# Typed rows as three bf16 terms, one-hots laid side by side, 11 of 24 groups gathered in the build, spread stores, out-degrees from a fourth product

## The chip, the cores and the metric

One core of a Trainium2 chip runs the whole program in one launch. The metric is the device time of one execution in microseconds (us); lower is better.

## The reference

A graph network of four layers runs over 6,250 nodes with 128 features and 206,250 edges, which come sorted by destination. An edge has a source, a destination, one of 3 types, a weight and 64 features of its own.

```
L0: agg  = [relu(x), for t in 0..2: segment_sum(relu(x[src] @ W_e[t].T + b_e[t]) where type == t, dst)]
    x    = layernorm(x + (agg @ W_n[ntype].T + b_n[ntype]) + x)
L1: sup  = proj(mobius_add(logmap0(x) @ W, bias));  agg = segment_sum(edge_weight * sup[dst], src)
    x    = layernorm(x + proj(expmap0(agg)))
L2: deg  = segment_sum(1, src) + 1
    x    = layernorm(x + x / deg + segment_sum(rsqrt(deg[src] * deg[dst]) * x[src], dst))
L3: agg  = segment_sum(edge_attr @ W_edge + x[src], dst) * deg_in ** -0.5
    x    = layernorm(x + relu(agg @ W + bias))
```

## The kernel before

Nodes are cut into NB = 49 blocks of 128. The sums over edges are made in two ways. For L1 to L3 the kernel **builds** the adjacency once, plain in bf16 (`adj`) and weighted in float32 (`wadj`), in DRAM, and multiplies with it. For L0 and the edge features it goes over the edges in **groups**. The stages follow one another, each with its own order on each engine:

**Up to 287 us**: loads, in-degrees by a histogram (DVE one-hots in `hist_hot`, L317 and L318; PE products), and the fields of every edge (key, destination, weight, source, ...) written to `edge_fields`.

**Table stage, 287 to 569 us** (L892 to L1063). First the out-degree histogram of the sources: 101 batches (`outs`, L948 to L951), 44 of them ahead of everything (`AHEAD`), the rest shared out over 62 blocks. Then per block n (62; the first 49 carry typed messages): POOL fetches the block's edge fields by one gather (`took`, L919), ACT copies slot and weight (L998) and DVE picks valid slots (L966), PE transposes three tables, ACT evicts them as bf16 (L1005), DVE splits the weight in three bf16 parts, and SP stores `slot_tabs` (L899, 160 KB). PE multiplies a block of x with the three W_e (L1036 to L1040), ACT applies relu (L1015), and SP stores 128 rows of `typed_msgs` (3 x 128 float32).

**Build, 569 to 2199 us** (L1066 to L1173). A block is 8 batches of 16 slices; there are 62 blocks, 496 batches. A slice is a product of two one-hots over 128 edges: slot (128 columns) by source block (49 columns), once plain and three times times a weight part. Per batch DVE makes them in five operations (L1132 to L1137: `hi`, `lo`, `hi` times w1, w2, w3), all laid [4 slice groups][column][4 slices], so that PE's operands (L1155 to L1157) have a stride of four elements (8 bytes). PE does 3 products a slice: 98 columns (plain and w1), 49 (w2), 49 (w3). ACT evicts in two copies a batch (L1169, L1171). At a block's end SP stores `adj` (1568 KB) and `wadj` in four stores of 784 KB, each from 32 neighbouring partitions (L1107), then loads the next tables. POOL has nothing to do. Buffers are doubled by batch (one-hots, psum) and by block (stores).

**Edge stage, 2248 to 4427 us** (L1176 to L1327). There are NG = 856 groups of GE = 256 edges (U = 2 tiles of 128), in Q = 8 buffers; a group's rows all belong to one block of 128 destinations. SP loads a group's fields and features (L1255, L1257). POOL gathers its source rows of its type, one indirect DMA for 128 rows of 512 B (L1272). DVE makes the one-hots: 384 columns (type and destination) float32 for each tile (L1292) and 128 columns for the features (L1295), and adds the group's sums to `acc` (L1301) and `sum_e` (L1303). PE does two products of the features (L1315, float32, 128 columns) and two of the gathered rows (L1319, float32, 384 columns).

**The rest**: L0's node products and norm (to about 4704 us), the product with `wadj` for L1 (to 5362; its rows are `spread` over 4 by `spread_out`, L1543), two products with `adj` for L2 and L3 (L1743, 5436 to 6568), and the end at 6689.

Of the kernel before, what the change touches and what calls it, by code (L numbers as in the profile page):

```python
# [16 lines left out]
F32 = mybir.dt.float32  # L17
# [20 lines left out]
U, Q = 2, 8  # L38
GE = U * P
NG = -(-((E + NB * (GE - 1)) // GE) // Q) * Q  # L40
TP = NG * U
STEPS = NG // Q
# [15 lines left out]
KT = 8192  # L58
assert KT > NP + P
# [19 lines left out]
NO_ROW = OVR - 1  # L79
GB = JB + NB  # L80
# [4 lines left out]
HROW = AROW // S2  # L85

# [25 lines left out]
ROUNDS = 15  # L112
PEELED = NG // Q % ROUNDS


def in_groups(eng, step):

    for r in range(PEELED):
        step(r * Q)
    with eng.Fori(PEELED * Q, NG - ROUNDS * Q + 1, ROUNDS * Q) as g0:  # L120
        for r in range(ROUNDS):
            step(g0 + r * Q)


def build(nc, x, src, dst, attr, etype, weight, ntype, w_e, b_e, w_n, b_n, w1, b1, w3, w3e, b3, out):
    ctx = ExitStack()
    with ctx:
# [15 lines left out]
        typed_msgs = nc.dram_tensor("typed_msgs", (NP, T * D), F32, kind="Internal").ap()  # L143
        slot_tabs = nc.dram_tensor("slot_tabs", (GB * P, 5 * SLOTS), BF16, kind="Internal").ap()
# [14 lines left out]
        iota = sb("iota", T * P)  # L159
# [13 lines left out]
        start_of = sb("start_of", NG, I32, rows=1)  # L173

# [7 lines left out]
        ramp = sb("ramp", P * TU, BF16)  # L182
        big_words = (nc.sbuf_bytes_remaining // 4) // 16 * 16 - 64
# [69 lines left out]
        xTs, mrows = [room(D) for _ in range(2)], [room(T * D) for _ in range(2)]  # L253
# [48 lines left out]
        s_mst = sems("s_mst", 2)  # L302
# [35 lines left out]
        out_count = ps[5][:, 64:64 + NB]  # L338

        with nc.Block() as block:  # L340
            @block.sync
            def _(sp):
# [7 lines left out]
                for col, a in ((dst_i, dst), (src_i, src), (typ_i, etype), (w_c, weight)):  # L350
# [5 lines left out]
                sp.wait_ge(s_fillf, 9)  # L356
# [5 lines left out]
                sp.dma_start(by_place[E:BROWS, :].rearrange("(p u) r -> p (u r)", u=U),  # L362
                             fillf[0:(BROWS - E) // U, :]).then_inc(s_pads, 16)
# [5 lines left out]
            def _(pool):  # L369
# [3 lines left out]
                pool.iota(iota[:, :], pattern=[[KT, T], [1, P]], base=0, channel_multiplier=0,  # L373
# [6 lines left out]
                          allow_small_or_imprecise_dtypes=True).then_inc(s_cst, 1)  # L380
                pool.wait_ge(s_cst, 7)
# [117 lines left out]
            def _(dve):  # L499
# [9 lines left out]
                for f3, k in ((fillf.rearrange("p (u r) -> p u r", u=U), NO_NODE), (front.unsqueeze(1), -1)):  # L509
                    dve.memset(f3[:, :, KEY:DST + 1], float(k)).then_inc(s_fillf, 1)  # L510
# [32 lines left out]
                do(dve.scalar_tensor_tensor(F3[:, :, KEY], tmp, float(KT), F3[:, :, DST], ALU.mult, ALU.add))  # L543
# [331 lines left out]
        def slots_here(eng, n):  # L875
# [1098 lines left out]
```

## Time and profile before

| | |
|---|---|
| median of 3 runs | 6698.84 us (6689.83 to 6706.6) |
| profiled execution | 6690.94 us; its span 6689.2 us; granted clock 0.930 |
| PE busy | 5658.0 us (85%) |
| weight loads busy | 3702.9 us (55%) |
| DVE busy | 4679.1 us (70%) |
| POOL busy | 1809.4 us (27%) |
| ACT busy | 1031.0 us (15%) |
| DMA | 1028.57 MB, mean 154 GB/s |

The shares are means over stages with different limits: the build is full on PE and DVE while POOL is idle, and the edge stage has POOL at work and ACT idle. So it has to be read stage by stage.

### The profile page before, as it was taken

The numbers are of one execution on the slowest core, as the hardware profiler recorded it, in microseconds if no ns is written. First come the engines' busy times: TensorE is split into PE (matmuls) and PEld (weight loads), VectorE is DVE, ScalarE is ACT, GpSimd is POOL, SyncE is SP. The second block draws the span as 40 slices with busy tenths as digits, with TensorE's granted clock in tenths as the row PEclk, the third lists the DMA queues.
The fourth block names the chain that finished last, engine by engine and source line by source line (L and its number), as shares of the span: only waits on it lengthen the run. The fifth ranks groups of instructions, "written<-read, shape, count | busy, mean of one in ns | idle before, by whom it ended". The sixth has DMA issues, their size and how long they took to land. (4 is left out here: it accounts for less than half of the span.)

```text
span 6689.2 us, 122051 instructions
## 1 busy us (share of the span) xinstructions
PE 5658.0 (85%) x41983; PEld 3702.9 (55%) x41983; DVE 4679.1 (70%) x10318; ACT 1031.0 (15%) x1894; POOL 1809.4 (27%) x1887
## 2 busy tenths in 40 slices
PE   4398999999999688888888888874899959968896
PEld 3257999999999444444444444443555524433344
DVE  7789999999999788888888888868566650032003
ACT  0044444444444000000000000013000010000000
POOL 0011000000000477777777777720000002000200
PEclk5578999999999899999999999997999979989996
DMA  9555777777777433333333333340888737635862
GB/s 316 148 170 170 192 189 193 184 196 191 190 193 185 111 82 83 82 83 83 83 83 82 82 82 83 80 35 0 324 306 304 283 119 192 192 124 193 190 203 69
DMA packets 559193, 1028.57 MB, mean 154 GB/s; under 512 B 187721, under 2 KB 447710, under 8 KB 549578
## 3 DMA queue, kind: packets, MB, share of 16 engines
q1 hardware_dynamic: 486760, 872.14, 44.0%
q0 software_dynamic: 65392, 145.28, 9.7%
q10 hardware_dynamic: 6622, 6.38, 0.3%
q8 instruction: 162, 2.65, 0.2%
q14 instruction: 257, 2.11, 0.1%
HBM read 688.67 MB, written 387.65 MB: 161 GB/s over the span
## 5 line engine op out<-in xcount | busy, mean ns | idle before, releaser
L1272 POOL DMA_INDIRECT big<-typed_msgs,big x1712 | 1644.7, 961 | 2220.2 <-DMA big<-edge_fields 1729.8
L1319 PE MATMUL psum<-big 128*128 128x384 f32 x3424 | 1343.8, 515 | 331.0 <-DMA big<-typed_msgs,big 328.9
L1155 PE MATMUL psum<-big 128*128 128x98 bf16 x7936 | 1549.0, 272 | 49.2 <-DVE big L1137 38.2
L1156 PE MATMUL psum<-big 128*128 128x49 bf16 x7936 | 1535.7, 229 | 0.2 <-issue 0.2
L1157 PE MATMUL psum<-big 128*128 128x49 bf16 x7936 | 1534.8, 230 | 0.0
L1743 PE MATMUL psum<-big 128*128 128x512 bf16 (+1 forms) x4704 | 1003.1, 376 | 186.8 <-DMA big<-adj 186.8
L1319 PEld LDWEIGHTS psum<-big 128*128 128x128 f32 x3424 | 583.7, 190 | 756.6 <-DMA big<-typed_msgs,big 502.0
L1155 PEld LDWEIGHTS psum<-big 128*128 128x128 bf16 x7936 | 933.3, 118 | 104.1 <-DVE big L1137 78.3
L1156 PEld LDWEIGHTS psum<-big 128*128 128x128 bf16 x7936 | 945.1, 119 | 0.0
L1157 PEld LDWEIGHTS psum<-big 128*128 128x128 bf16 x7936 | 932.1, 117 | 0.3 <-issue 0.3
L1743 PEld LDWEIGHTS psum<-big 128*128 128x128 bf16 x4704 | 463.3, 99 | 721.9 <-DMA big<-adj 191.9
L1580 PE MATMUL psum<-big 128*128 128x416 f32 x1984 | 656.2, 494 | 61.5 <-DVE big L1614 60.8
L1292 DVE TENSOR_SCALAR big<-iota,big 128x384 f32<-128x384 f32 x1712 | 667.6, 430 | 2.4
L1315 PEld LDWEIGHTS psum<-big 128*64 128x64 f32 x3424 | 353.0, 136 | 535.5 <-issue 465.6
L1315 PE MATMUL psum<-big 128*64 128x128 f32 x3424 | 561.0, 287 | 64.9 <-DVE big L1295 52.8
L1133 DVE TENSOR_TENSOR big<-ramp,big 128x2048 bf16<-128x2048 bf16 x496 | 604.7, 1219 | 0.0
L1295 DVE TENSOR_TENSOR big<-iota,big 128x256 f32<-128x256 f32 x856 | 363.4, 425 | 335.2 <-PE psum L1319 329.9
L1614 DVE STREAM_TRANSPOSE big<-big 128x3136 f32<-128x3136 f32 x124 | 427.2, 3445 | 238.5 <-PE psum L1580 221.6
L1580 PEld LDWEIGHTS psum<-big 128*128 128x128 f32 x1984 | 378.0, 191 | 339.2 <-issue 82.3
L1169 ACT CAST big<-psum 128x784 bf16<-128x784 f32 x496 | 402.9, 812 | 870.0 <-PE psum L1157 870.0
L1790 POOL DMA_INDIRECT big<-spill,spill_row x98 | 92.5, 943 | 1502.0 <-DMA spill<-big 1472.7
L1301 DVE TENSOR_TENSOR big<-psum,big 128x384 f32 x856 | 471.6, 551 | 10.6 <-PE psum L1319 5.7
(294 smaller groups left out, 4630.4 us busy)
## 6 DMA issues: line engine op xcount, KB each, us to landing
wadj<-big SPq DMA_DIRECT2D x248, 784.0 KB, 13.0
big<-wadj SPq DMA_DIRECT2D x124, 1568.0 KB, 7.2
big<-adj SPq DMA_DIRECT2D x210, 896.0 KB, 4.7
adj<-big SPq DMA_DIRECT2D x62, 1568.0 KB, 5.3
big<-edge_feats SPq DMA_DIRECT2D x856, 64.0 KB
edge_feats<-in_edge_attr SPq DMA_DIRECT2D x1, 51562.5 KB, 163.2
big<-typed_msgs,big POOLq DMA_INDIRECT x1712
big<-edge_fields SPq DMA_DIRECT2D x856, 8.0 KB
```

Of the source, the lines that this page charges most:

```text
L1133: dve.tensor_tensor(lo_b[:, q, :, :, :], ramps(0, P), along_t(sl, P), ALU.is_equal)
L1155: pe.matmul(to[:, 0:2 * NB], lo, hi_b[:, q, g, :, u], start=True, stop=False)
L1156: pe.matmul(to[:, NB:2 * NB], lo, w2_b[:, q, g, :, u], start=False, stop=False)
L1157: last = pe.matmul(to[:, NB:2 * NB], lo, w3_b[:, q, g, :, u], start=False, stop=True)
L1272: pool.indirect_dma_start(out=got4[:, h, u, :], out_offset=None, in_=typed_rows, in_offset=bass.IndirectOffsetOnAxis(ap=fld4i[:, h, u, IDX ...
L1292: dve.tensor_scalar(hot4[:, h, u, :], iota[:, :], rel3[:, 0, h, u:u + 1], None, ALU.is_equal)
L1301: dve.tensor_tensor(to, ps[h][:, 0:T * P], to, ALU.add)
L1315: pe.matmul(ps[h][0:FE, T * P:(T + 1) * P], feat4[:, h, u, :], hotd4[:, h % LAG, u, :], start=(u == 0), stop=(u == U - 1))
L1319: last = pe.matmul(ps[h][:, 0:T * P], got4[:, h, u, :], hot4[:, h, u, :], start=(u == 0), stop=(u == U - 1))
L1580: last = pe.matmul(ps[c][:, 0:(b1 - b0) * 32], rows, turned[:, n % RT, q * QROW + b0 * 32:q * QROW + b1 * 32], start=(m == 0), stop=(m == ...
L1614: dve.transpose(turned[:, n % RT, :].rearrange("p (h i) -> p h i", i=32), wring[:, n % RW, :].rearrange("p (h g) -> p h g", g=32)).then_in ...
L1743: last = pe.matmul(ps[c % 2][:, 0:len(blocks) * P], terms_[:, k, b * D:(b + 1) * D], ring_a[:, m % RA, 0:len(blocks), s * P:(s + 1) * P], ...
```

## The change

**Sizes.** Groups have 512 edges (U = 4), in Q = 6 buffers; there are NG = 456 groups, in 19 turns of 24.

```diff
-U, Q = 2, 8
+U, Q = 4, 6
...
+TURN = 4 * Q
...
-KT = 8192
...
+STAGED = 11
+SPER = 7
+SROW = U * TERMS * D // 2
...
+
+
+def is_staged(pos):
+
+    return pos % 2 == 1 and pos < 2 * STAGED
+
 GB = JB + NB
...
-        typed_msgs = nc.dram_tensor("typed_msgs", (NP, T * D), F32, kind="Internal").ap()
-        slot_tabs = nc.dram_tensor("slot_tabs", (GB * P, 5 * SLOTS), BF16, kind="Internal").ap()
+        typed_msgs = nc.dram_tensor("typed_msgs", (NP, T * TERMS * D // 2), F32, kind="Internal").ap()
+        slot_tabs = nc.dram_tensor("slot_tabs", (GB * P, 2 * 5 * SLOTS), BF16, kind="Internal").ap()
...
-                    sp.dma_start(slot_tabs[n * P:(n + 1) * P, :], tabs[:, n % 2, :, :].rearrange("p r g -> p (r g)")
+                    sp.dma_start(slot_tabs[n * P:(n + 1) * P, :], tabs[:, n % 2, :, :, :].rearrange("p r g c -> p (r g c)")
                                  ).then_inc(s_slot_st[n % 2], 16)
```

**Table stage.** The out-degree histogram goes. A typed row is written as three bf16 terms (768 B): ACT writes relu in float32 and then the high term, DVE the rest, ACT the middle term, DVE the last. Slot tables hold every value twice (320 KB a block).

```diff
-        AHEAD = 44
-        shares = [(AHEAD + (HB - AHEAD) * n // GB, AHEAD + (HB - AHEAD) * (n + 1) // GB) for n in range(GB)]
...
-                outs(0, AHEAD)
...
-                    part = [tabs[:, k, r, :] for r in (2, 3, 4)]
...
-                    link(dve.tensor_tensor(rest, w, part[0], ALU.subtract))
-                    link(dve.tensor_copy(part[1], rest))
-                    dve.tensor_tensor(part[2], rest, part[1], ALU.subtract).then_inc(s_slot_w, 1)
+                    link(dve.tensor_tensor(rest, w, part[0][:, :, 0], ALU.subtract))
+                    link(dve.tensor_copy(part[1], rest2))
+                    dve.tensor_tensor(part[2], rest2, part[1], ALU.subtract).then_inc(s_slot_w, 1)
...
+                def rest(b):
+                    dve.wait_ge(s_m_hi, b + 1)
+                    dve.tensor_tensor(mrest3[b % 2], mfull3[b % 2], mterms[b % MR][:, :, 0, :], ALU.subtract).then_inc(s_m_rest, 1)
+
+                def last(b):
+                    dve.wait_ge(s_m_mid, b + 1)
+                    dve.tensor_tensor(mterms[b % MR][:, :, 2, :], mrest3[b % 2], mterms[b % MR][:, :, 1, :],
+                                      ALU.subtract).then_inc(s_m_last, 1)

                 for n in range(GB + 1):
+                    if 4 <= n < NB + 4:
+                        last(n - 4)
+                    if 3 <= n < NB + 3:
+                        rest(n - 3)
                     if n < GB:
...
-                    act.copy(tabs[:, k, 0:3, :], ps[k][:, 0:3 * SLOTS].rearrange("p (r g) -> p r g", r=3)).then_inc(s_slot_e, 1)
+                    act.copy(tabs[:, k, 0:3, :, :].rearrange("p r g c -> p (r g) c"),
+                             ps[k][:, 0:3 * SLOTS].unsqueeze(2).to_broadcast([P, 3 * SLOTS, 2])).then_inc(s_slot_e, 1)
...
+                    at_least(act, s_m_rest, b - 1)
+                    act.activation(mfull[b % 2], ps[6 + b % 2][:, 0:T * D], ACT.Relu).then_inc(s_me, 1)
+                    act.wait_ge(s_me, b + 1)
+                    act.copy(mterms[b % MR][:, :, 0, :], mfull3[b % 2]).then_inc(s_m_hi, 1)
+
+                def middle(b):
+                    act.wait_ge(s_m_rest, b + 1)
+                    act.copy(mterms[b % MR][:, :, 1, :], mrest3[b % 2]).then_inc(s_m_mid, 1)
...
-                    outs(*shares[n])
```

**Build.** One-hots lie [slice][column], so that PE's operands are contiguous; DVE works on pairs of columns, and the hot operands have 50 columns (NE) in place of 49. A fourth product a slice (`sources`, 49 columns) sums the out-degrees in psum bank 7. Psum is handed over in halves of 8 slices, so ACT does 4 copies of 392 columns a batch. Each of the four `wadj` stores reads 32 partitions with a stride of 4. POOL gathers the typed rows of 7 groups for every pair of blocks (28 gathers, 868 in all; `fields_part` loads their fields, 7 loads), and SP stores them to `staged` in two parts (`store_part`, 2.75 MB a pair in rows of 3072 B).

```diff
             c, at = cut(at, 2 * n * TT // 2)
-            return c.bitcast(BF16).rearrange("p (k g c t) -> p k g c t", k=2, g=TG, t=TU), at
+            return c.bitcast(BF16).rearrange("p (k t c) -> p k t c", k=2, t=TT), at
...
+        def in_pairs(hot):
+
+            return hot.rearrange("p t (c r) -> p t c r", r=2)
...
                     for k in range(2):
...
-                                         wadj_st[h * 32:(h + 1) * 32, k, :, :, :].rearrange("p q s g -> p q (s g)")
+                                         wadj_st[h::4, k, :, :, :].rearrange("p q s g -> p q (s g)")
...
+                            sp.dma_start(tab[:, k, :, :, :].rearrange("p r g c -> p (r g c)"),
...
+                        if k == 0:
+                            store_part(sp, i, 0)
+                            if not final:
+                                fields_part(sp, i + 1, 0)
...
+                        at_least(pool, s_sgot, i * (16 * SPER * U) + 16 * c0 * U)
+                        pool.wait_ge(s_sfld[h], i * (16 * (c1 - c0)) + (fld_from[h] + 16 * (c1 - c0)))
+                        at_least(pool, s_sst[h], i * 16 + sst_from[h])
+                        pool.sem_inc(s_turn, 1)
+                        for c in range(c0, c1):
+                            for u in range(U):
+                                pool.indirect_dma_start(
+                                    out=sgot4[:, c, u, :], out_offset=None, in_=typed_rows,
+                                    in_offset=bass.IndirectOffsetOnAxis(ap=sfld4i[:, c, u, IDX0:IDX0 + 1], axis=0)
+                                ).then_inc(s_sgot, 16)
...
-                            dve.tensor_tensor(lo_b[:, q, :, :, :], ramps(0, P), along_t(sl, P), ALU.is_equal)
...
+                            dve.tensor_tensor(in_pairs(lo_b[:, q, :, :]), ramp_to(0, P), along_slots(sl, P), ALU.is_equal)
...
-                            dve.tensor_tensor(hi_b[:, q, :, NB:2 * NB, :], hi, along_t(w1_, NB), ALU.mult)
...
+                            dve.tensor_tensor(in_pairs(hi_b[:, q, :, NE:2 * NE]), hi, along_slots(w1_, NE), ALU.mult)
+                            dve.tensor_tensor(in_pairs(w2_b[:, q, :, :]), hi, along_slots(w2_, NE), ALU.mult)
+                            dve.tensor_tensor(in_pairs(w3_b[:, q, :, :]), hi, along_slots(w3_, NE), ALU.mult).then_inc(s_hot_b, 1)
...
                 block_pairs(dve, body)
+                dve.wait_ge(s_mm_b, 2 * NBATCH)
+                dve.tensor_copy(outdeg, sources).then_inc(s_clear, 1)
...
+                            for h in range(2):
+                                at_least(pe, s_adj_e, n * 2 + (h - 1))
+                                for t in range(h * HT, (h + 1) * HT):
+                                    to = made_in(h)[:, t % HT, :]
+                                    lo = lo_b[:, q, t, :]
+                                    pe.matmul(sources, lo, hi_b[:, q, t, 0:NB],
+                                              start=isinstance(n, int) and n == 0 and t == 0,
+                                              stop=isinstance(n, int) and n == NBATCH - 1 and t == TT - 1)
+                                    pe.matmul(to[:, 0:2 * NE], lo, hi_b[:, q, t, :], start=True, stop=False)
+                                    pe.matmul(to[:, NE:2 * NE], lo, w2_b[:, q, t, :], start=False, stop=False)
+                                    last = pe.matmul(to[:, NE:2 * NE], lo, w3_b[:, q, t, :], start=False, stop=True)
+                                last.then_inc(s_mm_b, 1)
```

**Edge stage.** 11 groups of a turn of 24 are loaded whole by SP from `staged`; POOL gathers for the other 13 (988 gathers in all). DVE makes `relative` for two groups at a time (3 operations, each waiting for the one before), one one-hot of 1536 bf16 in pairs and one of 512 float32 a group, and one add of 512 columns (`sum_e` has become a part of `acc`). PE does 4 float32 products of the features and 12 bf16 products of 384 columns (3 terms for each of 4 tiles) a group. One-hots are kept for 2 groups (HS = 2), sums are taken LAG = 2 groups later.

```diff
+                            for h in range(2):
+                                act.wait_ge(s_mm_b, i * (4 * BATCHES) + (k * (2 * BATCHES) + 2 * b + h + 1))
+                                c0 = b * TT + h * HT
+                                act.copy(adj_st[:, k, :, c0:c0 + HT], made_in(h)[:, :, 0:NB].rearrange("p t s -> p s t"))
+                                act.copy(wadj_st[:, k, b // 2, :, c0 % 32:c0 % 32 + HT],
+                                         made_in(h)[:, :, NE:NE + NB].rearrange("p t s -> p s t")).then_inc(s_adj_e, 1)
...
+                        if is_staged(pos):
+                            sp.dma_start(got[:, h * SROW:(h + 1) * SROW],
+                                         staged[bass.ds(i * (STAGED * P) + pos // 2 * P, P), :]).then_inc(s_pre[h // 2], 16)
...
+                    for pos in range(TURN):
+                        if is_staged(pos):
+                            continue
...
+                def relative(i, pos):
+                    h = pos % Q
+                    two = slice(h, h + 2)
...
+                    node = node0[:, bass.ds(i * TURN + pos, 2)].unsqueeze(2).to_broadcast([P, 2, U])
+                    dve.tensor_tensor(rel3[:, two, :], fld4[:, two, :, DST], node, ALU.subtract).then_inc(s_rel, 1)
...
+                    dve.tensor_scalar(rel3[:, two, :], rel3[:, two, :], -1.0, float(P), ALU.max, ALU.min).then_inc(s_rel, 1)
...
+                    dve.tensor_tensor(relk4[:, two, :, :], rel3[:, two, :].unsqueeze(3).to_broadcast([P, 2, U, 2]),
+                                      fld4[:, two, :, KEY].unsqueeze(3).to_broadcast([P, 2, U, 2]), ALU.add).then_inc(s_rel, 1)
...
+                    h, k = pos % Q, pos % HS
+                    at_least(dve, s_mm, i * TURN + (pos + 1 - HS))
+                    dve.tensor_tensor(hot4[:, k, :, :].rearrange("p u (c r) -> p u c r", r=2),
+                                      ramp_pairs.unsqueeze(1).to_broadcast([P, U, T * P // 2, 2]),
+                                      relk4[:, h, :, :].unsqueeze(2).to_broadcast([P, U, T * P // 2, 2]), ALU.is_equal)
+                    dve.tensor_tensor(hotd4[:, k, :, :], iota[:, :].unsqueeze(1).to_broadcast([P, U, P]),
+                                      rel3[:, h, :].unsqueeze(2).to_broadcast([P, U, P]), ALU.is_equal).then_inc(s_hot, 1)
...
+                    to = acc[:, bass.ds(b * ACCW, ACCW)]
+                    dve.tensor_tensor(to, ps[h][:, 0:ACCW], to, ALU.add).then_inc(s_acc, 1)
...
-                            pe.matmul(ps[h][0:FE, T * P:(T + 1) * P], feat4[:, h, u, :], hotd4[:, h % LAG, u, :],
+                            pe.matmul(ps[h][0:FE, T * P:ACCW], feat4[:, h, u, :], hotd4[:, k, u, :],
                                       start=(u == 0), stop=(u == U - 1))
-                        pe.wait_ge(s_got[h], arrived(g0, 16 * U))
+                        got_wait(pe, i, pos)
                         for u in range(U):
-                            last = pe.matmul(ps[h][:, 0:T * P], got4[:, h, u, :], hot4[:, h, u, :],
-                                             start=(u == 0), stop=(u == U - 1))
+                            for r in range(TERMS):
+                                last = pe.matmul(ps[h][:, 0:T * P], got_terms[:, h, u, r, :], hot4[:, k, u, :],
+                                                 start=(u == 0 and r == 0), stop=(u == U - 1 and r == TERMS - 1))
...
-        spread = turned1.rearrange("p (b q l) -> p q b l", q=4, l=32)
+        spread = turned1.rearrange("p (b l q) -> p q b l", q=4, l=32)
```

## Rows read from the trace of the kernel before

**Rows 1.** The span in windows: us, then PE, PEld, DVE, ACT, POOL busy (instructions), PEclk, DMA share, GB/s.
```profile
287.00:361.00 74.00, 40.49 (x682) 34.46 (x683) 72.03 (x97) 1.45 (x4) 4.39 (x4) 0.50 0.57 126
361.00:569.00 208.00, 187.62 (x1369) 110.33 (x1366) 179.99 (x429) 98.77 (x280) 48.49 (x45) 0.76 0.67 208
569.00:2199.00 1630.00, 1579.46 (x23808) 1524.48 (x23808) 1553.21 (x2483) 761.36 (x992) 0.00 (x0) 0.99 0.71 187
2199.00:2248.00 49.00, 0.29 (x2) 0.29 (x3) 22.71 (x10) 0.00 (x0) 15.10 (x16) 0.51 0.50 132
2248.00:4427.00 2179.00, 1833.11 (x6848) 936.42 (x6846) 1764.06 (x5984) 0.00 (x0) 1629.65 (x1696) 0.99 0.34 81
```

**Rows 2.** Edge stage, groups by line: busy us, mean ns, idle us before and who ended it.
```profile
L1272 POOL DMA_INDIRECT big<-typed_msgs,big x1696 | 1629.6, 961 | 548.3 <-issue 459.4 <-DMA big<-edge_fields 62.5 <-PE psum L1319 26.4
L1319 PE MATMUL psum<-big 128*128 128x384 f32 x3424 | 1343.8, 515 | 331.0 <-DMA big<-typed_msgs,big 328.9
...
L1315 PE MATMUL psum<-big 128*64 128x128 f32 x3424 | 561.0, 287 | 64.9 <-DVE big L1295 52.8 <-DVE big L1303 9.9 <-issue 2.2
L1301 DVE TENSOR_TENSOR big<-psum,big 128x384 f32 x856 | 471.6, 551 | 10.6 <-PE psum L1319 5.7 <-issue 0.8
```

**Rows 3.** Edge stage, PE in order of time (start, us) where no gathered row was late.
```profile
2253.69 0.65 PE L1315 MATMUL psum<-big 128*64 128x128 f32 x4
2254.27 1.56 PE L1319 MATMUL psum<-big 128*128 128x384 f32 x4
2255.76 0.65 PE L1315 MATMUL psum<-big 128*64 128x128 f32 x4
```

**Rows 4.** First product with the stored adjacency, 60 us; columns as in rows 1.
```profile
5440.00:5500.00 60.00, 60.00 (x280) 27.20 (x279) 18.06 (x19) 5.68 (x6) 0.00 (x0) 1.00 0.64 206
```

**Rows 5.** Build, DVE in order of time: one batch and the next one's start.
```profile
575.63 0.55 DVE L1132 TENSOR_TENSOR big<-ramp,big 128x784 bf16<-128x784 bf16 x1
576.10 1.21 DVE L1133 TENSOR_TENSOR big<-ramp,big 128x2048 bf16<-128x2048 bf16 x1
577.23 0.56 DVE L1135 TENSOR_TENSOR big<-big 128x784 bf16<-128x784 bf16 x1
...
578.66 0.56 DVE L1132 TENSOR_TENSOR big<-ramp,big 128x784 bf16<-128x784 bf16 x1
```

**Rows 6.** Build, PE in order of time in the middle of it.
```profile
1000.04 0.26 PE L1155 MATMUL psum<-big 128*128 128x98 bf16 x1
1000.12 0.23 PE L1156 MATMUL psum<-big 128*128 128x49 bf16 x1
1000.17 0.24 PE L1157 MATMUL psum<-big 128*128 128x49 bf16 x1
1000.22 0.28 PE L1155 MATMUL psum<-big 128*128 128x98 bf16 x1
```

**Rows 7.** Build, the ACT group that evicts first; columns as in rows 2.
```profile
L1169 ACT CAST big<-psum 128x784 bf16<-128x784 f32 x496 | 402.9, 812 | 870.0 <-PE psum L1157 870.0
```

**Rows 8.** Build, two windows behind a block's last eviction; columns as in rows 1.
```profile
1000.00:1002.00 2.00, 2.00 (x32) 1.96 (x32) 1.86 (x3) 1.53 (x2) 0.00 (x0) 1.00 0.96 401
...
1008.00:1018.00 10.00, 9.88 (x151) 9.43 (x149) 9.63 (x16) 4.73 (x7) 0.00 (x0) 1.00 0.96 216
```

**Rows 9.** Gathers of the table stage and the one-hots beside them: ns min/median/max, first and last start.
```profile
L919 POOL DMA_INDIRECT big<-edge_fields,big x49: 936/1109/1305, 287.7 to 554.5; - x49
...
L317 DVE TENSOR_TENSOR big<-ramp,big x46: 1207/1214/1227, 402.8 to 565.8; 128x2048 bf16<-128x2048 bf16 x46
```

**Rows 10.** Table stage in order of time: ACT's first copy, DVE's first pick.
```profile
329.71 0.43 ACT L998 COPY big<-big 128x128 f32<-128x128 f32 x1 [79.82 <-DMA big<-edge_fields]
...
362.40 0.41 DVE L966 TENSOR_TENSOR big<-big 128x128 f32<-128x128 f32 x1
```

**Rows 11.** Table stage, ACT's eviction of the tables; columns as in rows 2.
```profile
L1005 ACT CAST big<-psum 128x384 bf16<-128x384 f32 x62 | 29.7, 479 | 103.6 <-DMA slot_tabs<-big 63.1 <-PE psum L1051 40.5
```

**Rows 12.** DMA issues: KB each, median us to landing.
```profile
slot_tabs<-big SPq DMA_DIRECT2D x62, 160.0 KB, 4.3
```

More of the change, by code:

```diff
@@ L109, in in_batches, with in_turns @@
         body(NB // BB, NB % BB)
[L112 to L122, printed above, removed]
+def in_turns(eng, body):
+    body(0)
+    with eng.Fori(1, NG // TURN, 1) as i:
+        body(i)
 def build(nc, x, src, dst, attr, etype, weight, ntype, w_e, b_e, w_n, b_n, w1, b1, w3, w3e, b3, out):
@@ L1200, in build, with before, got_wait @@
         s_kept = sem("s_kept")
[L1201 to L1205 removed]
+        s_pre = sems("s_pre", Q // 2)
+        def before(pos, staged):
+            return sum(is_staged(p) == staged for p in range(pos % Q, pos + 1, Q))
+        def got_wait(eng, i, pos):
+            mine = is_staged(pos)
+            per = before(TURN - Q + pos % Q, mine)
+            if mine:
+                eng.wait_ge(s_pre[pos % Q // 2], i * (16 * per) + 16 * before(pos, mine))
+            else:
+                eng.wait_ge(s_got[pos % Q], i * (16 * U * per) + 16 * U * before(pos, mine))
@@ L1207, in slot_free, with loaded_by @@
+        def loaded_by(i, pos):
+            return i * (16 * TURN // Q) + 16 * (pos // Q + 1)
         def slot_free(eng, done, g):
             at_least(eng, done, g + (1 - Q))
-        def registers(engine, table, first, n, most):
-            _, values = nc.values_load_multi_w_load_instructions(table[0:1, bass.ds(first, n)], engines=(engine,),
-                                                                 min_val=0, max_val=most,
-                                                                 skip_runtime_bounds_check_because="clamped where the table is made")
-            return values
@@ new lines, in turn @@
+                def turn(i):
+                    g0 = i * TURN
+                    opening = isinstance(i, int)
+                    for pos in range(TURN):
+                        if pos % Q == 0:
+                            skip = LAG if opening and pos == 0 else 0
+                            bucket = [None] * skip + list(registers(mybir.EngineType.DVE, bucket_of, g0 + (pos + skip - LAG),
+                                                                    Q - skip, NB - 1))
+                        if pos % 2 == 0:
+                            relative(i, pos)
+                        one_hot(i, pos)
+                        if bucket[pos % Q] is not None:
+                            add(g0 + (pos - LAG), (pos - LAG) % Q, bucket[pos % Q])
@@ L1307, in _ @@
+                in_turns(dve, turn)
+                bucket = registers(mybir.EngineType.DVE, bucket_of, NG - LAG, LAG, NB - 1)
+                for r in range(LAG):
+                    add(NG - LAG + r, (NG - LAG + r) % Q, bucket[r])
             @block.tensor
             def _(pe):
-                def step(g0):
-                    for h in range(Q):
-                        pe.wait_ge(s_hot, g0 + (h + 1))
-                        pe.wait_ge(s_feat[h], arrived(g0))
-                        slot_free(pe, s_acc, g0 + h)
+                pe.wait_ge(s_zero, 3)
```

292 lines of the change are left out of this document (163 added, 129 removed).

## The prediction

> **What bounds the kernel now.** I read the windows first: they show five stretches with five different limits [rows 1]. Then the groups by line of each stretch, then the engines in order of time.
>
> In the **edge stage** (2179 us, 856 groups, 2.55 us a group) no engine is full. The releasers say who is late: PE's typed products wait 329 us for gathered rows, and POOL waits for nothing but its own issuing [rows 2]. A gather costs POOL 0.961 us and, with 459 us over 1696 gathers, 0.27 us more; with small waits 2178 / 1696 = 1.28. Two a group are the 2.55 us. Where no row is late, PE shows its own pace: 0.58 us for two feature tiles, 1.49 for two typed tiles, 2.07 a group [rows 3].
>
> In the **build** (1630 us, 496 batches, 3.29 a batch) PE and DVE are both full [rows 1]. DVE's five operations follow each other in 3.03 us [rows 5]. A slice takes PE 0.18 us in order of starts [rows 6], and 1579 us / 7936 = 0.199 busy. ACT waits 870 us for PE [rows 7], so it has room; POOL is idle.
>
> In the **table stage** DVE is full (72 of 74 us, then 180 of 208) [rows 1], mostly with histogram one-hots, and the first block's fields lie there at 329.7 while DVE picks first at 362.4 [rows 10].
>
> **The change, part by part.**
>
> *Edge stage.* Typed rows in three terms turn 4 float32 tiles into 12 bf16 products of 384 columns. A bf16 product of 512 columns takes 60 / 280 = 0.214 us where PE is full [rows 4]; 384 columns are 0.161, 12 of them 1.93. Four feature tiles at 0.29 are 1.16. PE: 3.09, with 0.1 for the turn of semaphores 3.2 us a group of 512. POOL: 13 of 24 groups, 52 gathers a turn; at 1.23 to 1.28, say 1.26, 65.5 us, against PE's 24 x 3.2 = 76.8. That a gather of 768 B a row costs POOL what one of 512 B does is a choice; a turn holds up to 76.8 / 52 = 1.48 us a gather. DVE: 1536 bf16 at the 1.15 us of 2048 [rows 5] are 0.87; the 512-wide one-hot and add, by 0.551 for 384 [rows 2] and some 1 ns an element, 0.68 each; `relative` some 0.75 a pair: 2.6 a group. With HS = 2 a one-hot begins only when the group two back is done, but relative and one-hot together (2.3) fit in PE's 3.2. So PE sets the pace: 456 x 3.2 = 1459, **-720 us**. Ends: 3.09 (1409) and 3.4 (1550).
>
> *Build, DVE.* NE = 50 adds 16 elements to four operations, 0.03 us; the rest keeps its inner size. 3.03 + 0.03 + 0.04 for the changed waits is 3.10; 496 of them 1538, with 11 us of start and end 1549, **-81**. Lower end 3.06, upper 3.29 (lockstep as now).
>
> *Build, PE.* This asks for a slice in 3.10 / 16 = 0.194 us with a fourth product. Now the 98-column product holds the next start off for 0.08 and a 49-column one for 0.05 [rows 6]: about 1 ns a column, where a contiguous 512-column product has 0.42 ns [rows 4]. I put the difference down to the stride of four elements, which goes. Ends: 249 columns at 0.42 ns, 0.104 us, and today's 0.18 + 0.05 = 0.23 to 0.25. The forecast takes a value below 0.194.
> The Trainium skill, "SBUF — State Buffer", section "Door 1: The DMA port swizzle", speaks against this: a stride costs only where fewer than two accesses fall in a 16-byte line, so bf16 may be strided up to 8 elements for free. By that the present operands already run at full speed and the contiguous ones win nothing: the second end. No row shows one operand both ways; the rate of [rows 4] speaks against it, but that product is long and reads other weights.
>
> *Build, ACT.* Four copies of 392 for two of 784 (0.812 each [rows 7]), some 1.8 us of 3.1. Nothing.
>
> *Build, DMA.* Today a block's `adj` goes at 401 GB/s and its `wadj`, from 32 neighbouring partitions, at 216, with the queues 96% busy both times [rows 8]: 3.9 + 14.5 = 18.4 us of 26. With a stride of 4 over the partitions I take 401 for both: 4.70 MB in 11.7 us, a pair 23.5. New: 2.75 MB gathered, at 81 / 0.34 = 238 GB/s of busy queue [rows 1] 11.6; stored, 6.9; tables 1.6; fields 0.5. 44 of the pair's 49.6 us: tight, but covered. POOL: 28 x (1.109 + 0.30) [rows 9] = 39.5 of 49.6. Both cost nothing as long as they stay below.
>
> *DVE beside gathers.* The Trainium skill, "SBUF — State Buffer", section "Who interferes with whom", says that a DVE operation with two SBUF inputs and a GpSimd instruction that reads SBUF share a port, and the later of them blocks. In the table stage both kinds lay side by side: the one-hot of 2048 took 1.207 to 1.227, the gather 1.109 in place of 0.94 [rows 9]. So the trace has the gather some 0.17 longer and DVE untouched, and I charge DVE nothing.
>
> *Table stage.* The start comes 33 us earlier (329.7 for 362.4) [rows 10]. Per block the histogram's DVE share goes, two operations of 384 (some 1.1 us) come; ACT has its wider eviction (0.479 now [rows 11], some 0.86 then) and two more copies, about 3.0 us a block. The tables' two buffers decide: today ACT waits 63 us for their stores [rows 11], which land in 4.3 us for 160 KB [rows 12]. With 320 KB some 5.1, eviction, DVE's split, typed store ahead in the queue: about 8 us for two blocks. 49 x 4.0 + 13 x 3.65 = 243 us (208 now), so it ends at 573: **+4**. Ends: -33 (pace as now) and +45 (4.7 a block).
>
> *Around.* The drain before the edge stage has DVE's memsets (22.7 us) beside the last stores [rows 1]; these land sooner, -5. A memset of psum, the strided store of the feature sums and the strided spread of L1 give +6.
>
> **Sum.** -720 - 81 + 4 - 5 + 6 = -796. The profiled execution took 6690.9 (span 6689.2), so 5895; the median of the runs lies 8 above it: **5903 us**. All else (node products, L1 to L3) is untouched.
>
> **Rivals.**
> *1. The fourth product is not free.* PE needs 0.23 to 0.25 a slice, as the rule on strides has it: 16 x 0.245 = 3.9 to 4.1 a batch, 2034 us, so about 6400; in between (0.2 to 0.22) 5990 to 6150. For it: short products may have a fixed cost of 0.05 whatever their columns; rows can't exclude it. Against: the 98-column product takes longer than the 49-column one, so columns count. 12%.
> *2. The build is held by DMA.* If a stride over partitions gains nothing, a pair is 36.8 + 20.6 = 57.4 us, 31 x 57.4 = 1779, +241 on 1538: some 6145. Waits of ACT on its store buffers would show it. 8%.
> *3. The edge stage stays with the gathers.* At 1.6 us each, 52 are 83.2 a turn, 19 turns 1581: 6025. 7%.
> *4. Slower: gathers and DVE lock each other out in the build.* Place: DVE's five two-input operations beside 28 gathers a pair. Price: each gather holds DVE for its 1.08 us, 30.2 a pair, 79.8 x 31 = 2474, about 6839. It gives no gain from 796 / 868 = 0.92 us a gather on. Against it is the DVE row beside gathers [rows 9], though there one gather comes in 4 us, not in 1.8. 3%.
> *5. Pairs of columns cost DVE its pace.* If the broadcast pair runs at one element a cycle (about 1.07 ns an element for 0.55), a batch takes 6 us and the kernel 7400. Nothing in the trace has exactly this form; the inner run is two elements in place of four. 2%.
>
> **How the numbers follow.** Forecast (5815 to 5990: edge 3.09 to 3.4, table -33 to +45) 68%; the rivals 12, 8, 7, 3, 2. Low end 5815: PE at 3.09, table stage at its best. High end 6180: takes in rivals 2 and 3 and the lower half of 1; beyond it lie the rest of 1 and rivals 4 and 5, and the edges. A measurement tells 0.3%, 20 us, from no change. Faster 0.95, same 0.01, slower 0.04.
>
> **What would show it.** Right: a build batch of 3.10 us with DVE back to back and PE waiting for L1137's successor; L1107's successor landing in half its time for each byte; POOL in the build at some 39 us a pair with nobody waiting; edge groups at 3.2 with PE at 95% and hardly a wait for typed rows; the table stage ending near 573. Wrong: PE full in the build and DVE waiting for its one-hot buffers (rival 1); ACT waiting for stores of `wadj` (2); PE waiting for gathered rows at unstaged groups (3); DVE's one-hots longer than 1.25 us in the build (4), or twice their time throughout (5).

## The result and the profile after

The changed kernel takes 6349.6 us in the median of 4 runs (6296.4 to 6355.9), the kernel before 6697.3 in the same comparison: ratio 0.947, interval 0.942 to 0.951. Forecast were 5903 us, range 5815 to 6180. The sign was right and the size wrong: 348 us gained, 794 forecast. The profiled execution is the fastest one, 6296.4 us (span 6294.7). Two of the five jobs in which kernels were timed ran every kernel some 8% slower (the kernel before took 7260 and 7267 us there, 6697 to 6715 in the other three), so their times are not compared with the others.

The stretches of the changed kernel in windows, columns as in [rows 1]: the 43 us before PE starts and the table stage proper, then build, drain and edge stage.

```profile
282.00:325.00 43.00, 0.00 (x0) 0.00 (x0) 1.93 (x11) 0.52 (x2) 3.92 (x4) 0.50 0.97 208
325.00:563.00 238.00, 203.16 (x430) 91.90 (x430) 151.32 (x409) 161.33 (x381) 43.23 (x45) 0.50 0.73 249
563.00:2455.00 1892.00, 1184.82 (x31744) 1126.70 (x31744) 1539.28 (x2481) 866.15 (x1982) 1189.27 (x856) 0.86 0.74 258
2455.00:2525.00 70.00, 0.10 (x3) 0.00 (x0) 23.93 (x4) 0.87 (x2) 23.20 (x25) 0.50 0.68 176
2525.00:4021.00 1496.00, 1431.63 (x9120) 896.74 (x9120) 1095.85 (x2052) 0.00 (x0) 1156.76 (x976) 0.98 0.59 163
```

Against the forecast:

| stretch | before | forecast | after |
|---|---|---|---|
| up to the build | 569 | 573 | 563 |
| build | 1630 | 1549 | **1892** |
| drain, memsets | 49 | 44 | 70 |
| edge stage | 2179 | 1459 | 1496 |
| the rest | 2262 | 2268 | 2274 |

So the edge stage did nearly what was forecast (-683 of -720), and the build, which should have won 81, lost 262. Nothing in the build is full: PE is busy 63%, DVE 81%, POOL 63%, the queues 74%. It is a stretch of waits. DVE's own waits in it, as total, number and longest in us, sorted by what ended them:

```profile
DVE big L1249 <- PE psum L1280: 233.1, 113, 7.0
DVE big L1249 <- DMA big<-slot_tabs: 107.0, 6, 26.1
```

Together they are 340 us, and the build took 343 more than forecast: some two thirds are waits for PE, one third waits for tables. The work itself goes as fast as forecast. The batches of DVE, in order of time:

```profile
1041.91 0.57 DVE L1249 TENSOR_TENSOR big<-line,big 128x800 bf16<-128x800 bf16 x1
1042.40 1.22 DVE L1250 TENSOR_TENSOR big<-line,big 128x2048 bf16<-128x2048 bf16 x1
...
1044.51 0.57 DVE L1254 TENSOR_TENSOR big<-big 128x800 bf16<-128x800 bf16 x1
1048.87 0.57 DVE L1249 TENSOR_TENSOR big<-line,big 128x800 bf16<-128x800 bf16 x1 [3.79 <-PE psum L1280]
```

An undisturbed batch is 3.07 to 3.08 us (1041.91 less the start before it, 1038.84; forecast 3.10), where [rows 5] have 3.03. PE's slices, one with its fourth product:

```profile
1036.69 0.20 PE L1275 MATMUL psum<-big 128*128 128x49 bf16 x1
1036.72 0.20 PE L1278 MATMUL psum<-big 128*128 128x100 bf16 x1
1036.77 0.18 PE L1279 MATMUL psum<-big 128*128 128x50 bf16 x1
1036.79 0.18 PE L1280 MATMUL psum<-big 128*128 128x50 bf16 x1
1036.82 0.18 PE L1275 MATMUL psum<-big 128*128 128x49 bf16 x1
```

Four products start within 0.12 to 0.13 us where three took 0.18 [rows 6]: a 50-column product holds the next off for 0.02 to 0.03 us in place of 0.05, a 100-column one for 0.05 in place of 0.08. So a slice of four products is shorter than one of three was, and PE's arithmetic has room for the fourth. This fits a stride of four elements costing PE its rate; the moving operands and the weights lost it together, and no run separates the two. The Trainium skill, "SBUF — State Buffer", section "Door 1: The DMA port swizzle", has strides of up to 8 bf16 for free; this trace does not agree.

But 16 batches of 3.08 would be 49.3 us a pair of blocks. The median pair takes 58.2, and four take 74 to 95. Two things are behind this.

**PE stands in the middle of a slice, waiting for nothing that is recorded:**

```profile
1034.66 0.20 PE L1279 MATMUL psum<-big 128*128 128x50 bf16 x1 [1.69 <-issue]
```

**A gather runs for 37 us.** POOL, then DVE, then SP's queue of the changed kernel, in order of time on each:

```profile
809.70 37.04 POOL L1230 DMA_INDIRECT big<-typed_msgs,big  x1 [6.53 <-issue]
847.04 0.94 POOL L1230 DMA_INDIRECT big<-typed_msgs,big  x1 [0.31 <-issue]
```

```profile
805.82 0.58 DVE L1249 TENSOR_TENSOR big<-line,big 128x800 bf16<-128x800 bf16 x1 [0.39 <-PE psum L1280]
...
849.09 0.58 DVE L1249 TENSOR_TENSOR big<-line,big 128x800 bf16<-128x800 bf16 x1 [3.17 <-PE psum L1280]
...
892.42 0.58 DVE L1249 TENSOR_TENSOR big<-line,big 128x800 bf16<-128x800 bf16 x1 [24.77 <-DMA big<-slot_tabs]
```

```profile
824.20 1.14 SPq L1206 DMA_DIRECT2D big<-slot_tabs  x1
869.33 0.42 SPq L1157 DMA_DIRECT2D staged<-big  x1
872.35 2.59 SPq L1150 DMA_DIRECT2D big<-edge_fields  x4
875.20 0.35 SPq L1198 DMA_DIRECT2D adj<-big  x1
...
881.14 1.62 SPq L1206 DMA_DIRECT2D big<-slot_tabs  x1
```

Between 805.8 and 845.9 DVE had no pause (the next idle time ends at 849.09 and is 3.17 long), and the gather ended 0.8 us after that pause began. The remaining gathers of the part then took until 867.5; SP stood in `store_part` waiting for them, and behind that wait stood the next stores and tables. So DVE ran out of tables for 24.8 us. The profiled run has five gathers of over 15 us; another one of the same kernel, eight.

Two things hold for all 66 gathers of over 15 us in the five traces that have them (the changed kernel twice, experiment 1 below twice, experiment 8): each ends 0.81 to 0.83 us after DVE fell idle, and each is the first gather after POOL had stood still for 2.5 us or more. Gathers that follow the last one within 1 us (799 of the 868) took 2.0 us at most in the changed kernel, also where DVE ran without a pause: 1.15 to 1.32 us as a rule, against 0.94 to 0.95 with DVE idle. So DVE without a pause is needed for a lockout but is not enough for one; why the first gather alone is caught is not shown.

### The profile page after: what moved, and what is told of

Read it like the earlier page. It is cut to its first block and busy times, and to the rows that moved or that the text cites. A ratio compares the mean times of both kernels' runs of the same rounds, so it can differ in the third digit from the quotient of the medians.

```text
span 6294.7 us, 129529 instructions
## 1 busy us (share of the span) xinstructions
PE 4841.5 (77%) x50575; PEld 3217.3 (51%) x50575; DVE 3898.7 (62%) x6278; ACT 1202.4 (19%) x2984; POOL 2527.8 (40%) x2034
## 3 DMA queue, kind: packets, MB, share of 16 engines
q1 hardware_dynamic: 464788, 1072.53, 49.6%
## 5 line engine op out<-in xcount | busy, mean ns | idle before, releaser
L1275 PE MATMUL psum<-big 128*128 128x49 bf16 x7936 | 1131.4, 191 | 640.4 <-DVE big L1254 270.3
L1230 POOL DMA_INDIRECT big<-typed_msgs,big x868 | 1200.6, 1383 | 730.5 <-DMA big<-typed_msgs,big 432.2
L1386 POOL DMA_INDIRECT big<-typed_msgs,big x988 | 1168.1, 1182 | 346.7 <-issue 232.5
L1279 PE MATMUL psum<-big 128*128 128x50 bf16 x7936 | 1127.2, 197 | 69.8 <-issue 69.5
L1275 PEld LDWEIGHTS psum<-big 128*128 128x128 bf16 x7936 | 797.4, 100 | 692.6 <-issue 362.6
L1278 PE MATMUL psum<-big 128*128 128x100 bf16 x7936 | 1137.0, 216 | 1.2 <-issue 1.2
L1280 PE MATMUL psum<-big 128*128 128x50 bf16 x7936 | 1123.6, 190 | 6.6 <-issue 6.6
L1463 PE MATMUL psum<-big 128*128 128x384 bf16 x5472 | 987.4, 331 | 61.1 <-DMA big<-typed_msgs,big 61.0
L1280 PEld LDWEIGHTS psum<-big 128*128 128x128 bf16 x7936 | 840.5, 106 | 7.2 <-issue 7.2
L1279 PEld LDWEIGHTS psum<-big 128*128 128x128 bf16 x7936 | 798.1, 101 | 76.7 <-issue 76.6
L1886 PEld LDWEIGHTS psum<-big 128*128 128x128 bf16 x4704 | 464.0, 99 | 725.5 <-DMA big<-adj 192.9
L1278 PEld LDWEIGHTS psum<-big 128*128 128x128 bf16 x7936 | 799.6, 101 | 0.0
L1463 PEld LDWEIGHTS psum<-big 128*128 128x128 bf16 x5472 | 503.2, 99 | 447.8 <-issue 87.5
L1294 ACT CAST big<-psum 128x392 bf16<-128x392 f32 x992 | 482.3, 486 | 1034.0 <-PE psum L1280 980.4
L1416 DVE TENSOR_TENSOR big<-big 128x1536 bf16<-128x1536 bf16 x456 | 437.3, 959 | 373.3 <-PE psum L1463 371.0
L1250 DVE TENSOR_TENSOR big<-line,big 128x2048 bf16<-128x2048 bf16 x496 | 606.8, 1223 | 0.0
L1723 PEld LDWEIGHTS psum<-big 128*128 128x128 f32 x1984 | 377.9, 191 | 341.5 <-issue 82.5
```

Source lines behind the costliest of these rows:

```text
L1230: pool.indirect_dma_start(out=sgot4[:, c, u, :], out_offset=None, in_=typed_rows, in_offset=bass.IndirectOffsetOnAxis(ap=sfld4i[:, c, u, I ...
L1250: dve.tensor_tensor(in_pairs(lo_b[:, q, :, :]), ramp_to(0, P), along_slots(sl, P), ALU.is_equal)
L1275: pe.matmul(sources, lo, hi_b[:, q, t, 0:NB], start=isinstance(n, int) and n == 0 and t == 0, stop=isinstance(n, int) and n == NBATCH - 1 ...
L1278: pe.matmul(to[:, 0:2 * NE], lo, hi_b[:, q, t, :], start=True, stop=False)
L1279: pe.matmul(to[:, NE:2 * NE], lo, w2_b[:, q, t, :], start=False, stop=False)
L1280: last = pe.matmul(to[:, NE:2 * NE], lo, w3_b[:, q, t, :], start=False, stop=True)
```

## The experiments

Three theories of the build. **F**: PE's instructions are fetched anew in each turn of its loop, and late. **L**: gathers are locked out by DVE, and SP behind them holds the tables back. **D**: evictions wait for store buffers, because stores land late. For F there is a count of instruction packets (16 KB each) in the table of queues, of the build up to 2200 us (changed kernel first, then with PE's short loop):

```profile
q8 instruction: 270, 4.42, 1.2%
```

```profile
q8 instruction: 8, 0.13, 0.0%
```

The kernel before has 18 in its whole build; the changed one 303, ten for each turn of the loop.

Where 1, 3 and 4 have two expectations, the first belongs to a slow job, and so does the one of 2; only the mechanism is read from that job.

**1. PE's loop over one block in place of two** (512 products in its body for 1024).

```diff
-                    for k in range(2):
                         for b in range(BATCHES):
-                            n = i * (2 * BATCHES) + (k * BATCHES + b)
+                            n = i * BATCHES + b
...
-                block_pairs(pe, body)
+                body(0)
+                with pe.Fori(1, GB - 1, 1) as i:
+                    body(i)
+                body(GB - 1)
```

> The changed kernel, with only TensorE's own loop of the build cut: its body holds one block (8 batches, 512 products) in place of a pair (1024). Theory F (TensorE's instructions are fetched anew in each turn of the loop, and come late while the queues carry data): some 10 instruction packets a pair in the build fall to about none, the 8 to 9 us a pair in which VectorE waits for psum go, 31 x 8.4 = 260 us, so about 6090 in the profile, unless lockouts of the gathers grow, since VectorE then has fewer pauses. Theory D (evictions wait for their store buffers because stores land late beside the gathers): nothing changes, 6300 to 6350. Theory L (gathers are locked out by VectorE, SP waits for them and loads the tables late): four or more stalls of 22 to 29 us stay or grow in number.

> TensorE's loop of one block alone, as before. On the other chip it brought twelve gathers of 61 to 83 us and stalls of 40 to 67 us. Theory F alone: 8.4 us a pair less than the changed kernel, -260. Theory L with it: the pauses at the start of a pair, which TensorE's fetches gave VectorE, are gone, so lockouts come more often; 12 stalls of 45 us take 540 back: 6400 to 6600, slower than the changed kernel.

Measured: ratio to before 0.986 in the slow job, and **1.015** (6810.6 us) in the normal one, where the changed kernel itself had 0.948. The fetches are gone (8 packets), and with them DVE's waits for PE, 24 us in the whole build for the 233 above. Still the kernel is 446 us slower. Each gather as minimum, median and maximum in ns, for the changed kernel and then this one:

```profile
L1230 POOL DMA_INDIRECT big<-typed_msgs,big x868: 940/1153/37037, 564.7 to 2471.4; - x174
```

```profile
L1230 POOL DMA_INDIRECT big<-typed_msgs,big x868: 940/946/53960, 563.6 to 2974.2; - x174
```

21 gathers take over 15 us, and DVE waits 836 us for tables. One of them beside DVE:

```profile
995.50 48.10 POOL L1230 DMA_INDIRECT big<-typed_msgs,big  x1 [2.60 <-DMA big<-typed_msgs,big]
```

```profile
974.98 0.58 DVE L1249 TENSOR_TENSOR big<-line,big 128x800 bf16<-128x800 bf16 x1 [0.60 <-PE psum L1280]
...
1081.59 0.58 DVE L1249 TENSOR_TENSOR big<-line,big 128x800 bf16<-128x800 bf16 x1 [38.82 <-DMA big<-slot_tabs]
```

DVE fell idle at 1042.8, and the gather ended at 1043.6: it was let in when DVE had used up its tables. I expected 6400 to 6600; the lockouts cost more than that. In the changed kernel the pauses that ended the lockouts were DVE's waits for PE, as at 849.09 above; without them most lockouts last until the tables are used up.

**2. No gathers in the build** (all 24 groups are gathered in the edge stage).

> The changed kernel without any gathering in the build: all 24 groups of a turn are gathered in the edge stage. Edge stage: 96 gathers a turn at 1.25 us are 120 us, 19 turns 2280, 785 more than with staging. Build: theory L expects the stalls of over 20 us gone (about 100 us less); theory F expects most of the 8.4 us a pair to stay, so 31 x 57 = 1770; theory D expects both gone, 496 x 3.10 = 1540. Sum by F and L about 6296 - 120 + 785 = 6960, by D about 6730.

Measured in the slow job: 7370 us, ratio 1.016. DVE has no wait over 4 us inside the build, but a pair still takes 54.5, with 304 packets in the whole build. F and L both stand; D alone does not. The size of the edge stage (2755 us) can't be carried to a normal job.

**3. A memset of 16 elements a batch on DVE.**

```diff
-                            dve.wait_ge(s_hi_b, n + 1)
+                            dve.wait_ge(s_hi_b, n * 2 + 1)
+                            dve.memset(breather, 0.0).then_inc(s_hi_b, 1)
```

> The changed kernel with one small memset a batch on VectorE (16 elements, no input) in the build, between the one-hot of 2048 and the products with the weights. Theory L (a gather can be shut out as long as VectorE runs two-input operations without a pause): gathers of over 20 us and the stalls of 22 to 29 us for the tables go, -100, for 496 memsets of some 0.06 to 0.1, +30 to +50: 6230 to 6300. If a pause in which VectorE writes does not help: 6330 to 6400 with the long gathers still there. The 8.4 us a pair stay in any case.

> The small memset a batch alone. Theory L: no gather over 5 us, no stall over 20, -100 + 40: 6230 to 6300, with 8 us a pair of waits for TensorE left.

**4. Short loop and memset together.**

> TensorE's loop of one block and the small memset a batch together. If F and L are both right and the memset opens the port: batches of 3.10 + 0.08 us throughout, 496 x 3.18 = 1577, about 5980 to 6000 in the profile. If only F: as the run with the loop alone plus 40 us.

> Both. F and L together: a build of 496 x 3.15 to 3.2 = 1560 to 1590 and 5980 to 6030 in all, faster than each alone by over 200. If the build is then held by something else (stores landing late, theory D), 6100 to 6200 with VectorE and ACT waiting for stores.

**The changed kernel beside them:**

> The changed kernel itself, so that the next three have it on their own chip; the chip of the last four runs took 7260 us for the kernel before (6697 in the first comparison), and engines there wait for releases that no record shows. On a chip like the first: 6300 to 6360, with three to six gathers of over 20 us in the build. On one like the last: 7050 to 7200.

Measured in one normal job (before 6715.3):

| kernel | us | ratio to before, interval | build, first to last batch |
|---|---|---|---|
| changed | 6364.9 | 0.948, 0.946 to 0.950 | 1945 |
| short loop | 6810.6 | 1.015, 1.013 to 1.016 | 2390 |
| memset | 6253.8 | 0.931, 0.930 to 0.933 | 1845 |
| both | 6072.7 | 0.905, 0.903 to 0.906 | 1648 |

(In the slow job the memset alone had 0.970 and both 0.956.) With the memset no gather is longer than 2.0 us (the row is of both together; with the memset alone the longest is 1.98):

```profile
L1231 POOL DMA_INDIRECT big<-typed_msgs,big x868: 940/1167/2034, 563.4 to 2232.0; - x174
```

The two causes are not additive one by one: taking F away alone costs 445, L alone wins 100 of the build, both win 297. At DVE's own pace the build would take 496 x 3.09 = 1533 us; with both it takes 1648, 115 more. 92 of these are waits for tables, 23 waits for PE. So both together missed the 5980 to 6030 that were expected.

**5. The tables ahead of the block's stores in SP's queue**, on top of both.

> Loop and memset together, and SP loads the next tables before it stores the block (it waits for VectorE's last use of them, then for the evictions). With loop and memset alone VectorE waits 92 us for tables, 19 times, up to 18.8 each. If the tables are late because 4.7 MB of stores stand ahead of them in the queue: these go, 5970 to 6000. If they are late because SP itself still waits for gathers (store_part): little changes, 6040 to 6080.

Measured: 6061.0 us, ratio 0.904 (0.902 to 0.906), 12 us under "both" by two jobs whose kernels before differ by 12: no difference. DVE's waits for tables are gone, but ACT waits 142 us for `wadj` stores in their place: whichever comes first, the other is late. Neither of the two alternatives had this. For the last 100 us, stores that land late, as theory D has it, are what is left.

**6. Nine groups staged in place of eleven**, on top of 5 (STAGED = 9, SPER = 6, parts of 3 and 3).

> The last one with 9 of 24 groups staged in place of 11 (6 groups a pair of blocks in place of 7: 24 gathers). Build: 4 gathers (6 us of POOL) and 0.8 MB less a pair, the queues at 75% in place of 83%; the rest of VectorE's waits go: build 1550 to 1600. Edge stage: 60 gathers a turn x 1.25 = 75.0 us against TensorE's 78 (1484 / 19), so it stays at 1484 to 1500. Sum 5940 to 6000. If a gather in the edge stage costs more (1.35), it is held by them: 81 x 19 = 1540, and the sum is above the last one.

Measured: 6159.0 us, ratio 0.919. The build falls to 1561 as expected, but the edge stage (first to last one-hot) rises from 1484 to 1665 (87.6 us a turn, 1.46 a gather), by more than either alternative expected. PE's waits in the edge stage, nine staged, then the changed kernel:

```profile
PE psum L1468 <- DMA big<-typed_msgs,big: 175.2, 86, 4.2
```

```profile
PE psum L1463 <- DMA big<-typed_msgs,big: 61.0, 34, 3.8
```

**7. The spread of the wadj stores undone**, on top of "both" (`h * 32:(h + 1) * 32` and `(b q l)` again).

> Loop and memset together, with the spread undone: the wadj stores read 32 neighbouring partitions again. If these move 216 GB/s as in the kernel before: a pair needs 57 us of the queues, 31 x 57.4 = 1780 in the build for 1648, 6200 in all. If the spread gains nothing: 6073 as with it.

Measured: 6250.5 us, ratio 0.932 (0.930 to 0.934). The median pair takes 57.4 us, the price forecast for rival 2. The queues, 600 to 2100 us, "both" first, then without the spread:

```profile
600.00:2100.00 1500.00, 981.92 (x29504) 933.46 (x29504) 1423.32 (x2760) 805.34 (x1844) 980.84 (x790) 0.97 0.83 303
```

```profile
600.00:2100.00 1500.00, 931.05 (x26382) 890.04 (x26378) 1281.89 (x2475) 721.43 (x1651) 880.80 (x707) 0.91 0.92 272
```

Fuller and slower: the build takes 185 us more, the kernel 178 (the kernels before of the two jobs differ by 12).

**8. The changed kernel without its fourth product** (the out-degrees are left out and taken as zero), PE's loop over two blocks as in the change.

> The changed kernel without its fourth product (the out-degrees are left out and taken as zero); TensorE's loop still holds a pair, now 768 products as in the kernel before. Theory F by size of the loop's body: no fetches in the loop, as with the loop of one block, so VectorE's pauses go and the lockouts come: 6750 to 6820. If the fetches have another reason (the queues' load): 302 packets and 6330 to 6370 stay.

Measured: 6780.5 us, ratio 1.011. Instruction packets in the whole run fall from 374 to 88, PE's waits without a releaser are gone, and 20 gathers take over 15 us, the longest 69.7. It is the size of the loop's body that calls the fetches: 1024 products do, 768 don't. Taking work out of PE made the kernel 7% slower.

**9. What lets a gather in.** An addition of 16 elements with two SBUF inputs in the memset's place; and the memset in each fourth batch only; both with the short loop. The job was the second slow one (before 7266.9), so the times expected don't apply.

> TensorE's loop of one block, with an addition of 16 elements with two SBUF inputs in the place of the memset. If the gather gets in only where VectorE does not read a second input: as with the loop alone, gathers of 17 to 54 us, 6700 to 6830. If any short instruction in between gives it a turn: as with the memset, 6050 to 6090.

> TensorE's loop of one block, with the memset in each fourth batch only. If a gather that is shut out waits for the next input-less instruction: no gather longer than 4 x 3.1 + 1 = 13.5 us, several of 5 to 13, and a time near that with a memset in each batch, 6060 to 6150. If one memset helps only those gathers that happen to begin beside it: gathers of 20 to 50 us remain and 6300 to 6700.

```profile
L1231 POOL DMA_INDIRECT big<-typed_msgs,big x868: 940/1234/3792, 560.5 to 2686.5; - x174
```

```profile
L1231 POOL DMA_INDIRECT big<-typed_msgs,big x868: 942/949/8872, 563.4 to 2884.2; - x174
```

Measured: 0.929 and 0.952. With two inputs (the first row) no gather is longer than 3.8 us, with the memset in each fourth batch (the second) none longer than 8.9; in the other slow job the short loop alone had twelve of 61 to 83 us. So it is not the missing input that lets the gather in: a short instruction between the long ones is enough, with two inputs or none, and with fewer of them the longest wait grows. Why it is enough is not shown. Nor was a plain pause of DVE tried, so the instruction and the small gap around it are not told apart.

## Why the prediction was right and wrong

*Edge stage*: right within 37 us, in part by luck. PE takes 3.07 us a group (3.09 in the sum):

```profile
3000.28 2.12 PE L1463 MATMUL psum<-big 128*128 128x384 bf16 x12
3002.33 1.09 PE L1458 MATMUL psum<-big 128*64 128x128 f32 x8
3003.35 2.12 PE L1463 MATMUL psum<-big 128*128 128x384 bf16 x12
3005.40 1.09 PE L1458 MATMUL psum<-big 128*64 128x128 f32 x8
```

A turn takes 78.1 us (1484 / 19) where 24 x 3.07 are 73.7. The term that was mis-sized is "say 1.26" for a gather: with a mean of 1.185 busy (0.961 before) and 0.30 between two it is 1.49, at the limit of 1.48 that the forecast had named, so that 52 of them take about as long as PE. The rows of 768 B are not the reason: with DVE idle such a gather takes 0.945 us. Sorted by the operation that ran longest beside them, the 421 gathers beside the wide bf16 one-hot (L1416) took 1.45 us in the mean, those beside the float32 add (L1426) 0.98. In the kernel before, gathers beside the float32 one-hot with two inputs (L1295) took 0.96, so two inputs alone do not make a gather longer; whether the bf16 type or the operation's length does is not shown. The cover of 76.8 us for 65.5 that the forecast saw was no cover at all, as experiment 6 shows.

*Build, DVE*: 3.08 for 3.10, right. *Build, PE*: 0.12 to 0.13 a slice, below the 0.194 that were asked; the reason given, the stride, fits and is not isolated. Rival 1 is out. *ACT*: four copies at 0.49, 1.96 us for 1.8. *Spread*: behind a block's last eviction the queues now carry (window of the changed kernel) 382 GB/s, where 401 were forecast, and undone it costs what rival 2 said.

```profile
1017.00:1025.00 8.00, 5.62 (x177) 5.30 (x173) 8.00 (x14) 4.72 (x11) 4.99 (x5) 1.00 0.98 382
```

The forecast of the build failed at three places. The largest share, DVE's 233 us of waits for PE, comes from a term that was missing altogether; the other two explain the 107 us of waits for tables. **"Both cost nothing as long as they stay below"** (POOL's 39.5 and the queues' 44 of 49.6 us): the mean of POOL stayed below, but a gather was shut out for up to 37 us, and SP's queue, in order, made the tables wait for it. That is a wait added by the change ahead of an old transfer; I had summed the gathers but not followed what stands behind `store_part`. **"I charge DVE nothing"** was true of DVE and missed the other side: that a gather is 0.17 longer beside DVE [rows 9] was a sign that POOL is the one that waits. In the table stage DVE had pauses; in the build it can run 37 us without one, and a gather that began after a rest of POOL then waited for all of it. The Trainium skill, "SBUF — State Buffer", section "Who interferes with whom", lets the later of the two block until the first is finished; the gathers here waited over many DVE instructions, so the trace does not agree, and two-input additions in between set them free. Rival 4 had the right pair of engines and the wrong victim.

The missing term is the loop body: with the fourth product PE's loop is longer than what stays loaded. PE stood still 238 us in 122 stalls, DVE waited 233 us for it, and these waits in turn held the lockouts down (5 in this trace, 21 without them in experiment 1). The Trainium skill, "Advanced Engine Details and Errata", section "ISA Cache", gives TensorE 128 KB, in lines of 16 KB, which are 256 instructions. By that, an estimate, 1024 products with their 1024 weight loads fill all of it, and 768 don't; the packets of 16 KB and experiment 8 agree. I had counted the products' time and not their instructions.

*Drain*: -5 forecast, +21 measured. The last pair's gathers and their store come after DVE's last batch (the store is issued at 2489.6), and the memsets of 24 us after that. *Table stage*: 238 us for 243, which is luck: the forecast had the tables' two buffers decide, but their stores land in 3.7 us for twice the size (5.1 forecast), and ACT waits for them 18.5 us in all. The busiest engine is PE, 203 of 238 us at a granted clock of 0.50 (the lower level, 1.2 GHz), where the stage before had 0.76; the forecast had nothing on that, and what sets the pace is not shown. *The rest*: +12 for +6.

## What to carry to other kernels

An instruction added to an unrolled loop is paid for in loop body as well as in time: count the body before and after, and look at the instruction packets. Work given to an idle engine needs more than a mean below the bound: ask what locks it out, and which in-order queue waits for it ahead of something that the bound engine needs. Where two causes cover each other, removing one may make the kernel slower, so try them together: the short loop and one memset a batch bring this kernel to 6073 us, 0.905 of before, where each alone had 1.015 and 0.931.

## What the runs showed of the hardware

- A gather by POOL can be shut out by DVE for 17 to 70 us (61 to 83 in the slow job) while DVE runs bf16 operations with two inputs of 0.5 to 1.2 us without a pause; it ends 0.8 us after DVE's next pause. Only gathers that began after 2.5 us or more of rest on POOL were caught. An added instruction of 0.07 us (or 0.17 with two inputs) a batch ends this: 2.5 us at most with the memset, 3.8 with the addition.
- PE's loop of 1024 products with their loads was fetched anew in each turn, ten packets of 16 KB for a pair of blocks; loops of 768 or 512 products were not. PE stalled 238 us in 122 places, some 8 us a pair, the longest 7.3 us.
- With bf16 operands at a stride of 8 bytes PE took 0.18 us for a slice of 196 columns, 0.9 ns a column; with contiguous ones 0.12 us for 249, 0.5 ns.
- A gather of 128 rows costs POOL 0.94 to 0.95 us and 0.30 before the next with DVE idle, for rows of 512 B and of 768 B alike.
